# Attention with three products phases for eight scores instead of four, and one output copy per half

## The reference

```python
kqv = x @ W_kqv.T                                   # 16 heads of 16 features
score = jnp.einsum('bhsd,bhnd->bhsn', q, k) / 16 + slope_h * (n - s)
attn = jax.nn.softmax(score, axis=-1)               # over 1024 keys
out = jnp.einsum('bhsn,bhnd->bhsd', attn, v)
...
# FFN: 8 experts of 352, top 2 of a softmax router, weights normed and x 2.5, plus a shared SwiGLU of 704
return x + attention(xn) + ffn(xn)
```

## Time and profile before

| | |
|---|---|
| time, median of 3 runs | 2433.16 us (2431.81 to 2435.55) |
| profiled execution, its own time | 2423.83 us |
| its span | 2422.0 us |
| attention, first score to end | 1125.6 to 2422.0 us |
| busy, whole span | TensorE 97%, VectorE 78%, ScalarE 63%, GpSimd 38% |

### The profile page before, as it was taken

How to read it: one execution, slowest core, us unless ns; L and a number is a source line. 1 busy time by engine, 2 the same in 40 slices (tenths; PEclk the granted TensorE clock), 3 DMA queues, 4 the chain that set the end, 5 groups by cost and what they waited for, 6 DMA issues and landing times.

```text
span 2422.0 us, 53518 instructions
## 1 busy us (share of the span) xinstructions
PE 2358.2 (97%) x19110; PEld 1461.3 (60%) x19110; DVE 1896.9 (78%) x2827; ACT 1529.4 (63%) x3149; POOL 913.1 (38%) x1153
## 2 busy tenths in 40 slices
PE   8999999996999999989999999999999999999998
PEld 7888888885999999983333333333333333333333
DVE  6666666655556555559999999999999999999993
ACT  3333333333333333333888888888888888888887
POOL 2223332225242222210224454545454445444444
PEclk9999999998999999996999999999999999999999
DMA  6999866771232222215364647464646464646441
GB/s 193 182 164 176 176 139 149 140 131 31 78 105 75 76 75 75 77 53 89 63 98 83 111 76 111 76 111 77 109 79 111 76 111 76 111 76 112 76 76 51
DMA packets 247525, 245.55 MB, mean 101 GB/s; under 512 B 113452, under 2 KB 197036, under 8 KB 247256
## 3 DMA queue, kind: packets, MB, share of 16 engines
q1 hardware_dynamic: 222648, 188.54, 41.0%
q0 software_dynamic: 22448, 50.56, 9.7%
q10 hardware_dynamic: 2176, 3.02, 0.4%
HBM read 131.47 MB, written 93.66 MB: 93 GB/s over the span
## 4 chain that ended last, share of the span: by engine, by line
PE 52%; DVE 2%; ACT 1%; issue 0%; DVEq 0%
PE p L1426 27%; PE p_o L1438 23%; PE p L1418 2%; DVE neg L1296 2%; ACT probs L1398 1%; ACT o_sb L1388 0%; PE p L1450 0%; DVE att L1321 0%; DVE att L1341 0%; DVE rec L1318 0%; DVEq L1284 0%; DVEq L1295 0%
## 5 line engine op out<-in xcount | busy, mean ns | idle before, releaser
L1296 DVE TENSOR_REDUCE neg<-p 128x1 f32<-128x1024 f32 x1024 | 1240.7, 1222 | 38.5 <-PE p L1418 30.0
L1398 ACT ACTIVATE probs<-p 128x512 f32<-128x512 f32 x2048 | 1110.6, 597 | 192.2 <-PE p L1426 90.6
L1418 PE MATMUL p<-k_op,q_op 50*128 50x512 f32 x2048 | 766.1, 454 | 6.4 <-DVEq L1284 3.0
L1426 PE MATMUL p<-q_op,k_op 51*128 51x512 f32 x2048 | 751.0, 446 | 10.2 <-DVE neg L1296 5.7
L1438 PE MATMUL p_o<-probs,v_op 128*32 128x256 f32 x8192 | 655.2, 391 | 4.9 <-ACT o_sb L1388 0.5
L1426 PEld LDWEIGHTS p<-q_op,k_op 51*128 51x128 f32 x2048 | 305.4, 185 | 441.2 <-ACT probs L1398 364.0
L1438 PEld LDWEIGHTS p_o<-probs,v_op 128*32 128x32 f32 x8192 | 164.5, 108 | 375.9 <-ACT probs L1398 340.1
L1418 PEld LDWEIGHTS p<-k_op,q_op 50*128 50x128 f32 x2048 | 311.3, 189 | 27.5 <-DVE neg L1296 24.4
L829 POOL DMA_INDIRECT xe<-xn_scratch,ids x135 | 146.0, 1082 | 339.9 <-DMA ids<-lists_scratch 311.5
L1226 POOL COPY o_pl<-o_sb 128x512 uint16<-128x512 uint16 x63 | 38.8, 616 | 602.3 <-ACT o_sb L1388 602.3
L922 ACT ACTIVATE gated_e<-p_gate 128x352 f32<-128x352 f32 x135 | 62.7, 465 | 194.1 <-PE p_gate L860 109.1
(11 more groups left out here) (187 smaller groups left out, 4047.8 us busy)
## 6 DMA issues: line engine op xcount, KB each, us to landing
k_op<-qk_scratch SPq DMA_DIRECT2D x192, 128.0 KB
q_op<-qk_scratch SPq DMA_DIRECT2D x192, 128.0 KB
yr_scratch<-x SPq DMA_DIRECT2D x135, 128.0 KB
qk_scratch<-k_op SPq DMA_DIRECT2D x32, 512.0 KB
qk_scratch<-q_op SPq DMA_DIRECT2D x32, 512.0 KB
v_scratch<-v_op SPq DMA_DIRECT2D x16, 1024.0 KB, 13.0
v_op<-v_scratch SPq DMA_DIRECT2D x32, 512.0 KB, 11.5
x<-in_x SPq DMA_DIRECT2D x16, 512.0 KB, 4.9
```

Of the source, the lines that this page charges most:

```text
L1296: v.tensor_reduce(neg[half][:, col:col + 1], p1[use % 2][:], AX.XY, ALU.max, negate=True).then_inc(s["s1_read"], 1)
L1398: a.activation(probs[kb % 4][:, h], p2[use % 3][:], ACT.Exp).then_inc(s["s2_read"], 1)
L1418: return t.matmul(p1[use % 2][:, kh], q_op[u][lo:lo + S1_ROWS, pair, q0:q0 + P], k_op[u][lo:lo + S1_ROWS, pair, kh * 512:(kh + 1) * 512], ...
L1426: t.matmul(p2[use % 3][:], k_op[u][lo:lo + S2_ROWS, pair, kb * P:(kb + 1) * P], q_op[u][lo:lo + S2_ROWS, pair, half * HQ:(half + 1) * HQ], ...
```

## The change

- TensorE: of each eight scores (`SPAN`) the products phases stand behind l % 8 = 2 (side 1 of the block before last, 256 queries), 5 (both sides of the block before, 512 queries in all) and 7 (side 0 of the span's first block, 256). The phases of scores are so of 3, 3 and 2. The products work as a whole is the same.
- ScalarE: one copy of 512 queries per half, behind the exponential l = 5, in place of two of 256 behind l = 1 and 3. The semaphores `o_ok` and `pv_done` count accordingly, `pv_side` is gone. The first products of a half (now behind l = 7) wait for the copy.
- The last group takes its heads in the order 0, 1, 2, 3 in place of 0, 2, 1, 3, so that neighbouring scores lie on different rows of the array.
- GpSimd: two blocks are fetched in every even x_no, behind `rejoin`, and combined in the next odd x_no, in place of one block in each x_no. `last_batch` gathers two blocks in even x_no likewise. Even x_no are handled in the second half of a group.

```diff
-        OUT_COPY, OUT_SEEN = (1, 3), 1
+        OUT_COPY, OUT_SEEN = 5, 1
+        SPAN = 2 * GH
...
-                if x_no >= NK - 1:
-                    pool.wait_ge(s["att_ok"], x_no)
-                    combine(x_no - (NK - 1))
-                if NK - 2 <= x_no < first + NK - 2:
-                    fetch(x_no - (NK - 2))
+                block = x_no - x_no % 2 - (NK - 2)
+                mine = range(block, block + 2) if 0 <= block < first else ()
+                if x_no % 2:
+                    for n in mine:
+                        pool.wait_ge(s["att_ok"], x_no)
+                        combine(n)
                 rejoin(x_no)
-                if x_no < NK:
-                    last_batch(x_no)
+                if x_no % 2 == 0:
+                    for n in mine:
+                        fetch(n)
+                if x_no % 2 == 0 and x_no < NK:
+                    for q in range(2):
+                        last_batch(x_no + q)
...
+            def output_copy(x_no):
+
+                act.wait_ge(s["pv_done"], (x_no + 1) * NK + NK)
+                if x_no >= 2:
                     act.wait_ge(s["o_pl_ok"], x_no - 1)
-                cols = slice(side * SIDE, (side + 1) * SIDE)
-                a.copy(o_sb[half][:, cols], p_o[:, cols]).then_inc(s["o_ok"], 1)
+                a.copy(o_sb[x_no % 2][:], p_o[:]).then_inc(s["o_ok"], 1)
...
+            def products(block, side):
+
+                x_no, kb = divmod(block, NK)
+                u = x_no // 2 % 3
+                pe.wait_ge(s["s2_read"], block * GH + GH + 3)
                 if kb == 0 and side == 0:
-                    pe.wait_ge(s["o_ok"], 2 * (g * 2 + half) + 2)
-                if kb == NK - 1 and side:
-                    pe.wait_ge(s["o_ok"], 2 * (g * 2 + half) + 3)
+                    pe.wait_ge(s["o_ok"], x_no)
...
-                    if l % 2 and (n > GH or has_prev):
...
+                    block = (2 * g + half) * NK + l // SPAN * 2
+                    if l % SPAN == 2 and block:
+                        products(block - 2, 1)
+                    if l % SPAN == 5 and block:
+                        for side in range(2):
+                            products(block - 1, side)
+                    if l % SPAN == 7:
+                        products(block, 0)
```

More of the change, by code:

```diff
@@ L1082, in attend @@
         p_o = ps("p_o", [P, HQ])
-        names = ("passed ones_in init neg_set m_t_ok s1_ps s1_read s2_ps s2_read pv_done pv_side o_ok rec_ok "
+        names = ("passed ones_in init neg_set m_t_ok s1_ps s1_read s2_ps s2_read pv_done o_ok rec_ok "
                  "pool_c o_st0 o_st1 att_ok o_out base_in0 base_in1 yg_in0 yg_in1 fin_base fin_y "
@@ L1093, in attend @@
         MAX_UNITS = UNITS // 2
-        ORDER = (0, 2, 1, 3)
+        ORDER, LAST_ORDER = (0, 2, 1, 3), (0, 1, 2, 3)
         TURN_AFTER = (MAX_UNITS // 2, 0)
-        OUT_COPY, OUT_SEEN = (1, 3), 1
+        OUT_COPY, OUT_SEEN = 5, 1
+        SPAN = 2 * GH
         SIDE = HQ // 2
@@ L1221, in split @@
                 u = x_no % 2
-                pool.wait_ge(s["o_ok"], 2 * x_no + 4)
+                pool.wait_ge(s["o_ok"], x_no + 1)
                 if x_no >= 2:
@@ L1375, in _ @@
             act.sem_inc(s["s2_read"], 3)
-            act.sem_inc(s["o_ok"], 2)
             act.sem_inc(s["pv_done"], NK)
[L1379 to L1385, removed]
+            def output_copy(x_no):
+                act.wait_ge(s["pv_done"], (x_no + 1) * NK + NK)
+                if x_no >= 2:
                     act.wait_ge(s["o_pl_ok"], x_no - 1)
-                cols = slice(side * SIDE, (side + 1) * SIDE)
-                a.copy(o_sb[half][:, cols], p_o[:, cols]).then_inc(s["o_ok"], 1)
+                a.copy(o_sb[x_no % 2][:], p_o[:]).then_inc(s["o_ok"], 1)
             def group(g, u, turn, has_prev, has_next):
                 for n in range(UNITS):
-                    half, kb, h = n // HALF, n % HALF // GH, ORDER[n % GH]
+                    half, kb, h = n // HALF, n % HALF // GH, (ORDER if has_next else LAST_ORDER)[n % GH]
                     use = use2(g, n)
@@ L1398, in group @@
                     a.activation(probs[kb % 4][:, h], p2[use % 3][:], ACT.Exp).then_inc(s["s2_read"], 1)
-                    if n % HALF in OUT_COPY and (n >= HALF or has_prev):
-                        output_copy(*((g, 0) if n >= HALF else (g - 1, 1)), OUT_COPY.index(n % HALF))
+                    if n % HALF == OUT_COPY and (half or has_prev):
+                        output_copy(2 * g + half - 1)
                 if not has_next:
-                    for side in range(2):
-                        output_copy(g, 1, side)
+                    output_copy(2 * g + 1)
             groups(act, group)
@@ L1419, in max_half, with score @@
                                 k_op[u][lo:lo + S1_ROWS, pair, kh * 512:(kh + 1) * 512], start=True, stop=True)
-            def score(u, use, n):
-                half, kb, h = n // HALF, n % HALF // GH, ORDER[n % GH]
+            def score(u, use, n, order):
+                half, kb, h = n // HALF, n % HALF // GH, order[n % GH]
                 pair, x = divmod(h, 2)
@@ L1428, in score @@
                          start=True, stop=True).then_inc(s["s2_ps"], 1)
-            def products(g, u, half, kb, side):
+            def products(block, side):
+                x_no, kb = divmod(block, NK)
+                u = x_no // 2 % 3
+                pe.wait_ge(s["s2_read"], block * GH + GH + 3)
                 if kb == 0 and side == 0:
-                    pe.wait_ge(s["o_ok"], 2 * (g * 2 + half) + 2)
-                if kb == NK - 1 and side:
-                    pe.wait_ge(s["o_ok"], 2 * (g * 2 + half) + 3)
+                    pe.wait_ge(s["o_ok"], x_no)
                 cols = slice(side * SIDE, (side + 1) * SIDE)
@@ L1442, in products @@
                     ins.then_inc(s["pv_done"], 1)
-                elif kb == NK - 1:
-                    ins.then_inc(s["pv_side"], 1)
             def turn_output(g, half, use):
-                pe.wait_ge(s["o_ok"], 2 * (g * 2 + half) + 4)
+                pe.wait_ge(s["o_ok"], g * 2 + half + 1)
                 pe.wait_ge(s["s2_read"], use + 1)
@@ L1461, in group @@
                 nu, nt = following(u, turn)
-                read = lambda n: use2(g, n) + 4
                 for n in range(UNITS):
@@ L1476, in group @@
                         pe.wait_ge(s["s1_read"], use1 + 1)
-                    score(u, use, n)
+                    score(u, use, n, ORDER if has_next else LAST_ORDER)
                     if has_next:
@@ L1481, in group @@
                             ins.then_inc(s["s1_ps"], 1)
-                    if l % 2 and (n > GH or has_prev):
[L1484 to L1490, removed]
+                    block = (2 * g + half) * NK + l // SPAN * 2
[6 more added lines that the diff above has]
+                        products(block, 0)
                 if not has_next:
-                    pe.wait_ge(s["s2_read"], read(UNITS - 1))
+                    products(block, 1)
                     for side in range(2):
-                        products(g, u, 1, NK - 1, side)
+                        products(block + 1, side)
                     turn_output(g, 1, use2(g, UNITS))
```

## The result

The changed kernel takes 2488.73 us (median of 4 runs, 2486.55 to 2493.63) where the kernel before takes 2432.48 (4 runs, 2424.28 to 2435.55): ratio 1.0241, 95% interval 1.0223 to 1.0259. That is 56 us slower. The forecast was 2493, with a range of 2445 to 2520.

A forecast was written before the change was run, and what follows sets the result against it. The prediction took TensorE to bound the kernel before, and a buffer ring between TensorE and VectorE the changed one. +67 (ring), +2 (half boundaries) and -4 (last group) sum to +65, forecast 2493 us, range 2445 to 2520.

The forecast's parts named there:

- The pace before is TensorE's, 1.23 a round: Attention, kernel before: TensorE sets 1.23 us per two scores and one products phase; VectorE's floor is 1.14.
- The ring of 5.19: Buffer of scores 2 and 3, split by products: refill 2.92 plus two reduces 2.27, 5.19 us per eight scores, +67 us.
- The third score of a phase at 0.23: TensorE, changed kernel: a phase's third score follows the second after 0.23 us, as in a run; upper bound 0.33.
- The 512 phase at 1.34: TensorE's products phase of 512 queries, between scores 5 and 6: takes 1.34 us.
- TensorE's own 4.59: TensorE alone, three phases each of scores and products: 4.59 us per eight scores, 0.33 less than before.
- Rival 1: Splitting the pair of scores 2 and 3 costs nothing and TensorE's saving counts: -86 us, 2347 us; chance 0.08.
- The Trainium skill's rule: TensorE switches between scores and products drain it; by this alone eight scores get cheaper by one switch in and out.
- Half boundaries, +2: Between halves of a group: VectorE's reciprocal costs +0.19, two copies' delay of 0.16 goes, 62 times: +2 us.
- The irregular gap, no change: VectorE's wait of about 0.9 us once a group, at gathers and operand loads: no change, bounds -16 and +28 us.
- Last group, -4: Last group, without reduces: 39 us before, ScalarE's floor 33; -4 us, bounds 0 and -6.

The follow-up runs named there:

- the halved reduce: Each maximum taken over only the second 512 of 1,024 columns, in both kernels: changed kernel 2396.07 us (ratio 0.9870), kernel before 2407.11 us (0.9907).
- the old gathers: The changed kernel with the GpSimd part undone, one block fetched and combined in each x_no: 2496.07 us, ratio 1.0268.
- gathers-only kernel: The kernel before with only the GpSimd part of the change: 2433.2 us, ratio 1.0019.
- the kernel with pairs and order: The kernel before with blocks fetched in pairs, the last batch's gathers left alone, and head order 0, 1, 2, 3 in the last group: 2425.31 us, ratio 0.9990.

## Why the prediction was right, step by step

- *The pace before is TensorE's, 1.23 a round*: shown, by the halved reduce that left it alone. VectorE was busy 972 of 1,000 us in this stage (1300 to 2300), and this was no sign that it bound.
- *The ring of 5.19*: right to 0.01. The waits at the release (1.36), the exposed weights, 1.00 to score 3 and 0.57 to the reduce are all in the rows, and lengthening one term by 0.44 lengthened the octet by 0.43.
- *The third score of a phase at 0.23*: right (in the octet before the rows shown, scores 4 and 5 start at 1501.74 and 1501.98). *The 512 phase at 1.34*: 1.36.
- *TensorE's own 4.59*: wrong as a floor. With the ring open, the octet is 4.83, and the prediction let the score banks pass without a sentence. Rival 1 of the prediction, -86 us, could never have paid more than some 248 x 0.09 = 22 us, and the two kernels with the halved reduce lie only 11 us apart. It didn't touch the forecast, because the ring is above both; this is luck, not foresight.
- *The Trainium skill's rule* (TensorEngine Tiling (Array Packing), Key Properties) that a change of tiling mode drains the array: the trace agrees that a switch costs, about 0.1 us on each side. Of the 0.33 an octet that fewer switches and phases were to free, the run with the halved reduce showed 0.09. The rule says nothing of who waits for the refill, and that decided.
- *Half boundaries, +2*: the copy was hidden by the ring as worked out. In the first rows of TensorE above it starts 2.04 behind score 3 (1508.64 less 1506.60), and the products behind score 7 start 2.77 behind it (1509.37), where 2.04 and 2.78 were forecast; in the kernel before the wait for it is seen. But the reciprocal cost less: a group of 41.79 is eight octets of 5.20 and 0.19 over, so 0.10 a half and not 0.19. Against the 0.16 of the kernel before, that is 62 x -0.06, some -4 us.
- *The irregular gap, no change*: near by luck, as two terms that were left out nearly cancel. The pairs took most of the gap (a group 41.79 with them and 42.67 without), and slow stretches came into early groups (1181 to 1225 us: 44 us for a group, at a granted clock of 0.96; the clock of the whole run was 0.980, and 0.983 with the old gathers). The net is read from two sets of runs: 2488.73 with the new gathers, 2496.07 with the old, -7 us; the intervals of the two ratios overlap, so that its sign isn't shown by the times.
- *Last group, -4*: its octet is 4.6 us, first to last score 36.6 us against 38.8: -2.2.

The sum as measured: the phases, the copy and the order together 2496.07 - 2429.70 = +66 (with the old gathers; 58 to 72 by the interval), the gathers -7; the forecast was +65 for the first with nothing for the second. The boundaries (-4 for +2) and the gathers have the size of what the forecast had too much, 65 against 56, but the 56 is itself known to 54 to 63 only.

TensorE of the kernel after in the last group; the rows are the phases of three scores that begin two octets (2456.22 - 2451.63 = 4.59).

```profile
2451.63 0.83 PE L1426 MATMUL p<-q_op,k_op 51*128 51x512 f32 x3
...
2456.22 1.17 PE L1426 MATMUL p<-q_op,k_op 51*128 51x512 f32 x3
```

## What to carry to other kernels

When work is regrouped on an engine that passes buffers to another, count the ring through each buffer (release, refill, hand over, consume), not only the engine's own sum. A unit whose two parts are divided by other work costs that work in latency, even where the engine has time. Then look for the next limit before the saving is booked, here the banks. A shortened consumer (here the halved reduce) and a moved filler (the long products phase), both cheap edits, show at once whether a ring or an engine sets the pace.

## What was not expected of the hardware

Where GpSimd issues its gathers changes what other engines do. With eight in a row TensorE stood 1.69 us without a releaser in the trace, and the mean granted clock of the 48 us around it was 0.86, so that by my estimate some 13 us of them ran at 1.2 GHz in place of 2.4. With two gathers in each half VectorE had gaps of 0.9 us, and with four in every second half, away from the operand loads, no more than 0.54 (gathers-only kernel, from 1420 us on). A long row of gathers isn't enough for the fall of the clock: in the recorded execution of the kernel with pairs and order, six in a row (1281.90 to 1289.78) passed at 1.00. Why is open: no experiment separated the gathers' traffic from their issuing, or the gathers from the loads.
